# Weighting four states per GpSimd instruction, four softplus in one table visit, other buffer counts and another order, in a two-attention two-Mamba chain

## The reference

```
h[n] = h[n] * exp(dt * A[d, n]) + (dt * u) * B[n]
y    = sum over n of h[n] * C[n]
```

## Time and profile before

| | us |
|---|---|
| median of three runs | 1993.56 (1992.63 to 1994.8) |
| the profiled execution | 1993.47 |
| its span | 1991.7 |

### The profile page before, as it was taken

The page is one execution under the profiler, slowest core; times in us unless marked ns, Lnnn a source line. Parts: engine busy times, 40 slices in busy tenths (PEclk is TensorE's granted clock), DMA queues, the critical chain, the costliest instruction groups (busy, mean ns, idle before and its releaser), DMA issues. The chain is left out here.

```text
span 1991.7 us, 29252 instructions
## 1 busy us (share of the span) xinstructions
PE 1800.1 (90%) x9252; PEld 1254.2 (63%) x9252; DVE 1799.2 (90%) x2010; ACT 1709.4 (86%) x3224; POOL 1781.5 (89%) x775
## 2 busy tenths in 40 slices
PE   8979689998989999999999999898999999697778
PEld 7545455767666665757666575766757575555666
DVE  5559999999989999999989999999999999999983
ACT  3388788999989999999989999999989998868652
POOL 0059999999999999999999999999999999999970
PEclk9999799999999999999999999999999999898999
DMA  7035565555445545455545645555444545454630
GB/s 283 1 115 157 176 172 144 158 170 164 151 131 162 178 151 180 146 167 158 161 134 159 177 153 169 153 164 164 149 145 156 171 158 167 149 157 149 160 103 11
DMA packets 163785, 302.30 MB, mean 152 GB/s; under 512 B 18904, under 2 KB 27312, under 8 KB 162096
## 3 DMA queue, kind: packets, MB, share of 16 engines
q1 hardware_dynamic: 153110, 287.45, 47.5%
q10 hardware_dynamic: 10522, 12.99, 2.0%
HBM read 292.98 MB, written 5.29 MB: 150 GB/s over the span
## 5 line engine op out<-in xcount | busy, mean ns | idle before, releaser
L960 POOL TENSOR_TENSOR state<-state,c_rows 128x1024 f32<-128x1024 f32 x510 | 1200.0, 2396 | 25.5 <-DVE state L1588 16.6
L1588 DVE TENSOR_TENSOR_SCAN state<-decay,mix_banks 128x512 f32<-128x512 f32 x576 | 673.5, 1205 | 14.8 <-ACT decay L1294 0.7
L2023 PE MATMUL bank<-const_sb,state 128*128 128x128 f32 x4096 | 542.6, 280 | 45.1 <-POOL state L960 44.4
L2023 PEld LDWEIGHTS bank<-const_sb,state 128*128 128x128 f32 x4096 | 478.3, 144 | 156.9 <-issue 76.8
L1585 DVE TENSOR_TENSOR_SCAN state<-mix_banks,state 128x512 f32<-128x512 f32 x448 | 524.0, 1203 | 33.8 <-ACT mix_banks L1275 27.1
L951 POOL TENSOR_TENSOR state<-kept,b_rows 128x1024 f32<-128x1024 f32 x224 | 534.3, 2396 | 6.7 <-DMA b_rows<-flat_rows 4.0
L1294 ACT ACTIVATE decay<-kept,ssm_pack 128x512 f32<-128x512 f32 x576 | 396.3, 717 | 12.7 <-DVE state L1588 6.6
L1578 DVE TENSOR_TENSOR mix_banks<-kept,mix_banks 128x1024 f32<-128x1024 f32 x288 | 353.3, 1227 | 22.9 <-ACT mix_banks L1283 13.7
L1275 ACT ACTIVATE mix_banks<-kept,ssm_pack 128x512 f32<-128x512 f32 x448 | 302.2, 683 | 53.1 <-DVE state L1588 42.0
L1843 PE MATMUL bank<-kept,conv_diag 128*128 128x512 f32 x496 | 225.6, 593 | 0.0
L978 ACT ACT_TABLE_LOAD x165 | 211.7, 1283 | 8.6 <-issue 5.7
(11 more groups left out here) (206 smaller groups left out, 2212.0 us busy)
## 6 DMA issues: line engine op xcount, KB each, us to landing
b_rows<-flat_rows SPq DMA_DIRECT2D x512, 256.0 KB, 3.6
c_rows<-flat_rows SPq DMA_DIRECT2D x512, 256.0 KB, 3.7
conv_diag<-conv_diag SPq DMA_DIRECT2D x8, 1024.0 KB, 6.9
out<-x_res ACTq DMA_DIRECT2D x8, 512.0 KB, 4.2
ssm_pack<-ssm_pack SPq DMA_DIRECT2D x2, 1907.0 KB, 11.5
x_next<-x ACTq DMA_DIRECT2D x6, 512.0 KB, 5.2
x_again<-x_dbl ACTq DMA_DIRECT2D x16, 128.0 KB, 2.5
state<-ada_w SPq DMA_DIRECT2D x1, 1536.0 KB, 14.2
```

What stands on the lines that cost most here:

```text
L960: pool.tensor_tensor(st, st, by_pair(c_rows[:, row % ROWS]), ALU.mult).then_inc(m_prod, 1)
L1588: ins = dve.tensor_tensor_scan(st, decay[:, nth(g) % DECAYS], mixed, 0.0, ALU.mult, ALU.add)
L2023: ins = pe.matmul(y_banks[c2][:, t * P:(t + 1) * P], state[:, g % STATES, t * P:(t + 1) * P], ident, start=False, stop=(g == BANK_SUMS[g / ...
```

## The change

It raises the state ring to 16 slots and lets one POOL instruction weight four states, two pairs with their two C rows (255 in place of 510). The C row loads, the rewrite of `flat_rows` and the sums wait for weightings counted in fours. The decay buffers go from seven to five. The steps of the second half (`dt2`, `dt3`) move from `tail` into `before`, so that all four softplus of a scan follow one another; only for the first scan do they stay apart. The second half's dt of odd scans has a buffer of its own, `dt_late`. The tables of the order are all new; `KINDS`, `ROWS`, `C_BEHIND` and `LATE_PAIRS` are as before.

```diff
-BANKS, DECAYS, STATES, ROWS = 3, 7, 14, 4
+BANKS, DECAYS, STATES, ROWS = 3, 5, 16, 4
+WEIGHED = 4
-FIRST_BASES = {'att': (-53, -28), 'setup': -49, 'prep': -33}
-TAIL_BASE, POST_BASE, PREP_BASE = -17, -46, 9
-ATT_BASES, LATE_BASES = (18, 100, 152, 221), (41, 193)
+FIRST_BASES = {'att': (-54, -26), 'setup': -49, 'prep': -31}
+TAIL_BASE, POST_BASE, PREP_BASE = -1, -34, 9
+ATT_BASES, LATE_BASES = (13, 100, 152, 219), (44, 194)
...
-SETUP_STAGES = dict(zip(SETUP_NAMES, (2, 47, 25, 56, 77, 96, 80, 84, 121, 147, 73, 168, 176, 179), strict=True))
+SETUP_STAGES = dict(zip(SETUP_NAMES, (1, 21, 23, 36, 44, 69, 51, 62, 75, 87, 70, 91, 128, 139), strict=True))
...
-TAIL_FILLS = (("dt2",), ("dt3",))
-FIRST_PREP_FILLS = (("turn0", "x0", "x2", "v2", "xp", "dt0", "z0", "z2"),
-                    ("turn1", "x1", "x3", "v3", "dt1", "z1", "z3"))
+FIRST_PREP_FILLS = (("turn0", "x0", "x2", "v2", "xp", "dt0", "z0", "z2", "dt2"),
+                    ("turn1", "x1", "x3", "v3", "dt1", "z1", "z3", "dt3"))
...
-    "weight": range(0, ALL_UNITS - HC * LATE_PAIRS, HC),
+    "weight": range(0, ALL_UNITS - HC * LATE_PAIRS, WEIGHED),
...
+        dt_late = sb("dt_late", [P, HC, T])
...
+        def dt_half(si, h):
+            return dt_late[:] if h and si % 2 else dt[:, h * HC:(h + 1) * HC]
...
-                        past(sp, m_prod, si * HALVES * N + g + 1 - ROWS)
+                        past(sp, m_prod, ((si * HALVES * N + g + 1 - ROWS) * HC + WEIGHED - 1) // WEIGHED)
...
             def weight(g):
                 si, half, n, c2, c = split(g)
-                row = half * N + n
-                pool.wait_ge(c_loaded[row % ROWS], 16 * (si * (HALVES * N // ROWS) + row // ROWS + 1))
-                pool.wait_ge(m_scan, g + HC)
-                st = pair_states(g)
-                pool.tensor_tensor(st, st, by_pair(c_rows[:, row % ROWS]), ALU.mult).then_inc(m_prod, 1)
+                row, pairs = half * N + n, WEIGHED // HC
+                for k in range(row, row + pairs):
+                    pool.wait_ge(c_loaded[k % ROWS], 16 * (si * (HALVES * N // ROWS) + k // ROWS + 1))
+                pool.wait_ge(m_scan, g + WEIGHED)
+                st = state[:, g % STATES:g % STATES + WEIGHED, :].rearrange("p (n c) t -> p n c t", c=HC)
+                by_row = c_rows[:, row % ROWS:row % ROWS + pairs, :].unsqueeze(2).broadcast_to([P, pairs, HC, T])
+                pool.tensor_tensor(st, st, by_row, ALU.mult).then_inc(m_prod, 1)
...
                 for k, place in enumerate(dt_fills(si, h)):
                     at = h * HC + k
-                    yield from w.to(f"soft{at}")
+                    if k == 0 and (h == 0 or si == 0):
+                        yield from w.to(f"soft{at}")
                     table(SOFTPLUS)
                     src, done = filled(act, place)
-                    read_until = max(0, (si - 1) * UNITS + (h + 1) * HALF_UNITS)
+                    read_until = max(0, (si - 1 - h) * UNITS + (h + 1) * HALF_UNITS)
                     for kind in (BESIDE, SPREAD):
                         past(act, m_decay[kind], units_before(kind, read_until))
-                    act.activation(dt[:, at, :], src[:], ACT.Softplus,
+                    act.activation(dt_half(si, h)[:, k, :], src[:], ACT.Softplus,
                                    bias=sw(layer, "dt_b")[:, at:at + 1]).then_inc(done, 1)
...
                 yield from soft(w, pi, layer, 0)
                 if pi == 0:
                     yield from gates_copied()
                     yield from gates_activated()
+                yield from soft(w, pi, layer, 1)
                 yield from scaled(w, pi, layer, s, 0)
 
             def tail(si, layer, s):
                 w = Walk(TAIL_STAGES[si])
-                yield from soft(w, si, layer, 1)
                 yield from scaled(w, si, layer, s, 1)
...
                 steps(pi, layer, 0)
                 if pi == 0:
                     yield from project_gates()
+                yield from w.to("dt2")
+                steps(pi, layer, 1)
...
-                    pe.wait_ge(m_prod, g // HC + 1)
+                    pe.wait_ge(m_prod, g // WEIGHED + 1)
```

More of the change, by code:

```diff
@@ new lines @@
+    1: (124, 124, 126, 147, 152, 155, 156, 156, 156, 156, 158, 159, 161, 163, 171, 174, 178, 182, 182, 182, 182,
+        182, 182),
+    2: (121, 121, 122, 148, 148, 152, 162, 162, 162, 162, 166, 166, 170, 172, 174, 179, 185, 190, 191, 197, 206,
+        209, 212),
+    3: (129, 129, 130, 142, 145, 155, 155, 160, 160, 160, 164, 162, 169, 171, 174, 178, 184, 189, 194, 200, 206,
+        210, 218),
+    4: (124, 124, 126, 130, 151, 152, 153, 153, 153, 153, 153, 154, 154, 155, 160, 166, 172, 174, 174, 174, 174,
+        174, 174),
@@ new lines @@
+    5: (123, 123, 126, 132, 134, 152, 153, 153, 153, 153, 154, 154, 155, 157, 163, 169, 173, 176, 176, 176, 176,
+        176, 176),
+    6: (121, 121, 122, 135, 155, 154, 160, 163, 163, 163, 167, 167, 168, 173, 176, 182, 188, 191, 201, 205, 207,
+        210, 214),
+    7: (129, 129, 131, 132, 141, 156, 160, 163, 163, 163, 167, 167, 172, 173, 176, 186, 189, 196, 200, 205, 207,
+        216, 222),
+    8: (129, 129, 131, 135, 151, 153, 153, 154, 154, 154, 154, 154, 154, 155, 160, 166, 171, 174, 174, 174, 174,
+        174, 174),
@@ new lines @@
+    9: (122, 122, 126, 152, 153, 153, 155, 155, 155, 155, 157, 156, 160, 162, 168, 173, 177, 182, 182, 182, 182,
+        182, 182),
+    10: (122, 122, 126, 131, 132, 154, 157, 155, 155, 155, 162, 159, 168, 170, 173, 179, 184, 189, 192, 198, 204,
+         208, 210),
+    11: (130, 130, 130, 134, 136, 152, 157, 164, 164, 164, 167, 168, 171, 172, 175, 180, 186, 190, 195, 203, 208,
+         210, 214),
+    12: (121, 121, 126, 131, 150, 151, 152, 152, 152, 152, 153, 153, 153, 154, 157, 164, 170, 174, 174, 174, 174,
+         174, 174),
@@ L232 @@
[L232 to L244 removed]
+    0: (39, 41),
+    1: (2, 6),
+    2: (18, 21),
+    3: (2, 18),
+    4: (13, 19),
+    5: (16, 18),
@@ L245 @@
+    6: (13, 19),
+    7: (11, 19),
+    8: (2, 21),
+    9: (17, 20),
+    10: (16, 19),
+    11: (11, 19),
+    12: (2, 18),
+    13: (15, 18),
+    14: (3, 17),
+    15: (20, 24),
 })
-SETUP_STAGES = dict(zip(SETUP_NAMES, (2, 47, 25, 56, 77, 96, 80, 84, 121, 147, 73, 168, 176, 179), strict=True))
+SETUP_STAGES = dict(zip(SETUP_NAMES, (1, 21, 23, 36, 44, 69, 51, 62, 75, 87, 70, 91, 128, 139), strict=True))
 ALL_UNITS = SCANS * UNITS
@@ L250 @@
 STEPS = {
-    "bank": (7, 8, 1, 4, 9, 2, 7, 4, 8, 8, 8, 8, 9, 4, 10, 8, 3, 5, 4, 4, 1, 3, 8, 8, 7, 8, 10, 6, 4, 5, 8, 8, 11,
[13 rows of a table removed]
-    "row": (6, 9, 7, 4, 7, 6, 8, 8, 8, 3, 10, 13, 7, 6, 5, 10, 8, 8, 2, 4, 10, 8, 7, 4, 10, 8, 4, 7, 6, 9, 5, 8, 8,
[8 rows of a table removed]
-    "beside": (11, 9, 19, 22, 24, 25, 35, 13, 2, 5, 4, 7, 9, 12, 30, 33, 18, 19, 30, 33, 44, 26, 27, 29, 2, 5, 16,
[22 rows of a table removed]
-    "inject": (13, 28, 34, 27, 29, 29, 23, 4, 20, 29, 29, 25, 27, 10, 9, 16, 13, 10, 13, 14, 18, 23, 13, 22, 9, 11,
[8 rows of a table removed]
-    "weight": (9, 5, 8, 8, 9, 8, 6, 15, 11, 10, 10, 14, 13, 9, 9, 6, 7, 7, 10, 6, 7, 8, 6, 16, 13, 13, 13, 10, 9,
[19 rows of a table removed]
@@ L326 @@
[L326 removed]
[39 rows of a table removed]
[L366 to L368 removed]
+    "bank": (9, 4, 7, 1, 13, 1, 7, 7, 8, 8, 6, 8, 12, 5, 7, 6, 6, 8, 12, 8, 8, 6, 4, 6, 6, 8, 10, 2, 12, 5, 11, 6,
[13 rows of a table added]
@@ new lines @@
+    "row": (5, 9, 13, 6, 6, 4, 10, 8, 8, 4, 8, 10, 5, 5, 8, 12, 8, 8, 3, 4, 12, 5, 10, 3, 11, 8, 8, 7, 8, 12, 7, 6,
[8 rows of a table added]
+    "beside": (10, 2, 13, 14, 16, 19, 29, 17, 2, 5, 13, 7, 11, 13, 30, 30, 24, 22, 30, 23, 21, 22, 20, 18, 24, 27,
[21 rows of a table added]
+    "inject": (13, 27, 29, 24, 30, 22, 24, 13, 19, 21, 20, 15, 18, 11, 6, 16, 16, 7, 25, 20, 22, 9, 16, 14, 13, 12,
[8 rows of a table added]
+    "weight": (14, 16, 16, 18, 16, 20, 15, 15, 16, 19, 20, 16, 21, 17, 24, 23, 20, 22, 15, 21, 21, 24, 19, 22, 20,
[10 rows of a table added]
+    "sum": (38, 35, 31, 28, 26, 23, 21, 18, 22, 25, 24, 23, 40, 38, 35, 33, 46, 43, 40, 38, 35, 33, 30, 28, 28, 27,
[39 rows of a table added]
+}
@@ L407, with fill_at @@
 ATT_FILL = att_bank_counts()
-def fill_at(names, what, preps, tails, posts):
+def fill_at(names, what, preps, posts):
     bank = 0 if what in names[0] else 1
@@ L413, in fill_at @@
     in_first = len(FIRST_PREP_FILLS[bank]) - len(PREP_FILLS[bank]) if preps else 0
-    before = in_first + len(PREP_FILLS[bank]) * preps + len(TAIL_FILLS[bank]) * tails + len(POST_FILLS[bank]) * posts
+    before = in_first + len(PREP_FILLS[bank]) * preps + len(POST_FILLS[bank]) * posts
     return bank, before + names[bank].index(what)
@@ L810, in dt_fills @@
         def dt_fills(si, h):
-            return [(tail_fill if h else prep_fill)(si, f"dt{h * HC + k}") for k in range(HC)]
+            return [prep_fill(si, f"dt{h * HC + k}") for k in range(HC)]
+        def dt_half(si, h):
+            return dt_late[:] if h and si % 2 else dt[:, h * HC:(h + 1) * HC]
```

(10 more changed lines are left out.)

124 lines of the change are left out of this document (63 added, 61 removed), and 377 rows, old and new, of tables (ATT_STAGES, PREP_NAMES, PREP_STAGES, STEPS).

## The result

The changed kernel takes **2000.86 us** (median of five runs, 2000.01 to 2004.84), against 1993.56 before (five runs, 1992.63 to 1994.96). The ratio is 1.0048, 95% interval 1.0032 to 1.0063. The forecast was 1963 with a range to 1998: the kernel became 7 us slower where 31 us less were forecast. The profiled execution after is 2000.86 us, its span 1997.9, so 6.2 us of the difference lie inside the span: the first injection comes at 113.38 us where it came at 112.41 (+1.0), from there to the start of DVE's last weighting it is 1821.9 us where it was 1816.6 (+5.3), and the rest has its old length.

What follows compares the result with a forecast made beforehand. The prediction took POOL to bound the loop, with DVE close behind. From 1993.5 us, -35 (DVE's limit, with 38 off POOL) and +4 (start) made -31, so 1963 us, range 1936 to 1998.

Steps and rivals of the forecast that it cites:

- What bounds the kernel now: Reading of the loop's busy shares: bound by POOL at 97.8%, with DVE close behind at 94.7%.
- DVE's limit: Loop: DVE's unchanged 1719.7 us of work at 96.5% busy gives 1782 us, 35 us less than now.
- Part 1: POOL's weightings: 510 become 255, saving 0.15 us of fixed cost each, 38 us off POOL.
- Part 2: Softplus on ACT: four in one visit, 30 table loads fewer, 38 us off ACT, priced at 0.
- Part 3: Five decay buffers: priced 0, end +30 us; 16 state slots: 0 to +5 us.
- Part 4: Delays behind the larger weighting: +4 us at the loop's start, 0 at the end, 0 for later B row loads.
- SP's queue: Row loads: half the B rows issued up to 3.5 us later, priced 0; as a slower rival 2014 us, chance 0.10.
- Part 5: The new order, with setup products of later layers moved ahead: 0, ends -4 and +4 us.
- DVE was the bound already: Rival: POOL's relief becomes waiting for scans, the loop keeps its length, 1991 to 1997 us; chance 0.12.
- the memset's price: Rival: a weighting's fixed part is only a memset's, POOL loses 10 us, total 1987 us; chance 0.12.
- The chance of slower: Two slower rivals: late B rows, 2014 us, chance 0.10; DVE waiting for decays, 2018 us, chance 0.05.

Runs made afterwards that it cites:

- a_pairs: The changed kernel with two weightings of pairs, back to back, in place of each weighting of four states; 2005.34 us, 1.0067 of the kernel before.
- a_split_pairs: The changed kernel with pairs weighted in place of fours and the third and fourth softplus 8 quarter units behind the first two; 2008.75 us, 1.0080 of before.
- a_split: The changed kernel with the third and fourth softplus placed eight quarters of a unit behind the first two; 2006.09 us, 1.0075 of the kernel before.
- b_soft: The kernel before with four softplus of the later 15 scans in one visit, where the second stood; 2041.89 us, 1.0256.
- a_room_d5: The changed kernel with the last attention layer using the first one's weights, five decay buffers and 16 slots kept; 1.0039 of the kernel before.
- b_noload: The kernel before with an exponential computed for each softplus, so 62 table loads fewer; 1.0001.

## Why the prediction was wrong

**What bounds the kernel now** is the step that failed: "The loop is bound by POOL, with DVE close behind." I read 97.8% against 94.7% as an order of rank, with 3% between the first and the second. The gap is there in busy time and not in time: 28 us off POOL in the unchanged order gave 1 us, some 5 at an equal clock. DVE's gaps were not slack that POOL could give it. My own sign for it, POOL down by 38 us and the span by under 10, came about: POOL fell by 34.9 us, and the span rose by 6.2. The sentence beside it, "The two are coupled; a faster POOL helps only as far as DVE can follow", was right, and I then let DVE follow by 35 us on the strength of bank waits that ACT's relief was to shorten.

**DVE's limit** failed with it, and it carried the sum. "At the 96.5% of its best long stretch that is 1782 us" took the share of one stretch for the share that the loop could reach. After, DVE has 1722.5 us in a loop of 1822.9, 94.5%, where it had 94.7. To reach 96.5% what DVE waits for would have to come earlier, and that is ACT's banks more than POOL's products, 40.8 us against 6.2. ACT had 41.5 us less to do, and these bank waits stayed as they were (34.9 and 36.1 us between 150 and 1850 us).

**Part 1** was right in kind and too large by a little: 255 instructions, 34.9 us off POOL in all where 38 were forecast, 0.137 us a piece by that and 0.105 to 0.125 by the rows, against 0.15. In the time it is worth some 4 us in the new order (`a_pairs`), 1 beside the four split visits (`a_split_pairs` against `a_split`), and perhaps nothing at an equal clock.

**Part 2** was near: 130 table loads where 135 were forecast, from 165, and 41.5 us off ACT for 38. It was priced 0 in itself. `a_split`, which undoes four of the fifteen visits, is 5 us slower, within the intervals, so the part's whole worth is open. What I left out is the wait inside the visit, 22 us in all, and that the visit, put where the old order had room for two softplus, costs 51 us (`b_soft`): who waits while no decay comes was the price to look for.

**Part 3** was priced by the wrong wait. For the decay buffers I took DVE's 0.7 us; the wait to look at is the writer's, ACT's for a free buffer, and what queues behind it. In the old order, together with ten more table loads from the moved decays, that is +47 us, beyond the end of +30 that I gave. In the new order the same wait is 16.4 us, where it was 6.6, and two more buffers change nothing. The slots: +22 us of waits for PE's sum, outside the 0 to +5, yet worth nothing, as 20 slots show.

**Part 4**: the start was near. The opening loses 1.3 to 2 units by 150 us, 2.4 to 3.5 us where 4 was forecast; the first product on the states comes at 114.40 after a wait of 12.0 us, against 112.55, and the first weighting after 4.84 us of waiting for scans. A part of this can be the clock of that one execution: over the first 100 us it was granted 0.88 in after and 0.91 before, and in the profiled executions of `a_room_d5` and `a_split`, where it was 0.93, the first injection comes at 109.73 and 108.08 us against after's 113.38. SP's queue was right: SP waits 1065.8 us for weightings where it waited 519.7, and POOL is short of B rows for 5.7 us against 4.0. A queue can wait twice as long and cost nothing.

**Part 5: "0, ends -4 and +4."** This is the other term that failed. The new order, with pairs again and four of the fifteen visits apart, costs 16 us (`a_split_pairs`). An order is not neutral because nothing in it has a price of its own. That it pays for sums that trail by 8.6 units and for a visit of 7.4 us is argued, not shown.

**The rivals.** "DVE was the bound already" (0.12) described the result best: POOL's relief turned into waiting, for scans (25 to 40 us, short of the 55 that I had set as its sign) and for slots (2 to 24), the loop all but kept its length, and 1991 to 1997 was 4 us short of the measured time. Its mechanism is still not the one: 26 us off DVE give 3, some 5 at an equal clock. SP's queue and the memset's price fell. The chance of slower, 0.14 (its two parts add to 0.15), went to causes that did not happen; the cause that did, an order with a price of its own, had no rival.

## What to carry to other kernels

When two engines are both above 94% in a fixed order and each waits now and then for the other, treat them as one resource, though this case makes that likely and doesn't show it: price what a change takes off both, and put a cut of one alone at a tenth to a fifth, until a cut of a few tokens in the unchanged order has measured it. Where the effect is a few us, compare the granted clocks of the executions as well as their times, and count the instructions of an experiment before reading its time: `a_split` undid four visits where fifteen were meant. A buffer count is priced by the waits of the engine that fills it and of what queues behind that wait, not by the reader's. And where a change needs a new order to work at all, the order is a term of the sum, to be bounded by a kernel with the new order and the old operations.

## What was not expected of the hardware

- The Trainium skill (Perfetto Trace Analysis, "Identifying the Most-Contended Engine") says to optimize the engine with the highest occupancy first. Here that was GpSimd in the loop, and 27.6 us taken off it gave 1 us, within its interval of nothing, and some 5 at an equal clock.
- ACT had 79 us less to do in `b_noload`, 4% of the time, and the time did not move (1.0001). Its executions had the lowest clock of the single cuts, 0.966.
- A product of 2048 elements per partition on GpSimd runs at 4.515 us from start to start and one of 1024 at 2.31, so the fixed part of 0.105 us is below that of 0.158 that the earlier trace rows give for DVE's product, the row from which I took mine.
